# Cross attention's layer norm computed inside the down projection before it, and the first batch's tiles loaded there

## The chip, the cores and the metric

One core of a Trainium2 chip runs the whole program. The metric is the device time of one execution in microseconds. The kernel before has a median of 2226.97 us in three runs (2225.14 to 2232.52).

## The reference

Eight batches of 256 tokens with 512 features pass through two gated blocks. Each block adds a gated attention and a gated feed-forward part to x. The change lies between the end of the first block and the start of the second:

```python
x = x + jnp.tanh(g_xattn[0]) * _L0_xattn_ref(_layernorm(x, axis=-1), ctx_2048, ...)
x = x + jnp.tanh(g_ffn[0]) * _L0_ffn_ref(_layernorm(x, axis=-1), L0_ffn_w_gate, L0_ffn_w_up, L0_ffn_w_down)
x = x + jnp.tanh(g_xattn[1]) * _L1_xattn_ref(_layernorm(x, axis=-1), ctx_2048, ctx_2048)
x = x + jnp.tanh(g_ffn[1]) * _L1_ffn_ref(_layernorm(x, axis=-1), L1_ffn_w1, ...)

def _layernorm(x, axis=-1, eps=1e-05):
    m = jnp.mean(x, axis=axis, keepdims=True)
    v = jnp.var(x, axis=axis, keepdims=True)
    return (x - m) / jnp.sqrt(v + eps)
```

`_L0_ffn_ref` ends in `h_sparse @ w_down`, 2048 features down to 512. `_L1_xattn_ref` is causal attention with 16 heads of 32 features: queries are the normalised x, keys and values both the context, and the scores are divided by sqrt(32).

## The kernel before, in words

Seven stages run one after the other. Each is a block with one program per engine, and an all-engine barrier closes it. Between stages x goes through DRAM. Batches are taken in four pairs of 512 tokens, which are 16 tiles of 128 tokens.

**The down projection (stage 5, `down` with tag `d_`, lines 1073 to 1319).** The loop goes over the 16 token tiles g. Two of the products were already computed in stage 4. For each of the 14 others ScalarE rounds the tile to its high part (L1270), VectorE takes the low part (L1302), and TensorE adds up 48 products of 128x128 by 128x512 (L258 to L260). VectorE then adds gate times product to x (`add`, L1286), and SyncE stores y (L1164). SyncE has the only DMA queue and works in program order: load tile g, load one piece of the weights of stage 7, store an old y, load an old x. Eight pieces of 1 MB pass through four buffers `raw`. ScalarE takes a piece's signs, VectorE sums its sizes (L1306), and TensorE turns the signs in between. GpSimd has nothing to do in this stage.

**The cross stage (stage 6, `cross`, lines 1633 to 2061).** A batch has 16 heads, taken as eight pairs p, and an engine's program is a chain of steps, one pair a step. In step p TensorE computes the scores of pair p (L1848, L1851), turns the probabilities of pairs p-2 and p-1 (L1860) and in even steps multiplies by the values (L1875). VectorE masks (L2008) and takes the maximum (L2012), ScalarE takes exp (L1937, L1939) and copies the turned probabilities out of PSUM (L1950). Two PSUM banks S hold scores, so the scores of pair p wait for the exps of pair p-2. Work on the neighbouring batches is hung into fixed steps: outputs of the batch before in steps 3 and 4 (L1885, L2033, then GpSimd's adds L1799), and for the batch after the statistics of its layer norm in step 2 (L192 to L197), its normalising in step 4 (L204) and its turning into queries in steps 5 and 6 (L1830, copied by L1930 and L1998). The power -1/2 of the variance is GpSimd's (L213).

Before the first step the stage loads the first batch's x (`x_xl`, L1747) and its keys (`x_kt`, L1750), normalises, turns and copies. TensorE first runs 12 throw-away products on the identity (`keep_awake`, L253) once x has landed, and 12 more in each of the first two steps. One such f32 product stands in the trace as two rows, so a dozen is x24. Ahead of all of it VectorE fills `x_masked` and the two whole score banks with a constant (L1989, L1991), and TensorE waits for that.

Of the kernel before, what the change touches and what calls it, by code (L numbers as in the profile page):

```python
# [1072 lines left out]
def down(nc, io, c, scr, tag, w, gate, x_from, x_to):  # L1073
# [4 lines left out]
    with ExitStack() as ctx:  # L1078
# [35 lines left out]
        if made:  # L1114
            SIGNS = 8
            AHEAD = 4
            raw = [mem.sb(f"raw{i}", [P, 4, 512]) for i in range(WP)]
# [4 lines left out]
            W = mem.bank("W")  # L1122
            v_arrived = [mem.sem(f"v_arrived{i}") for i in range(SIGNS)]
# [21 lines left out]
        def piece(n):  # L1145
            return raw[n % WP][:].rearrange("p k n -> p (k n)")

        @block.sync
        def _(sp):
# [16 lines left out]
            def load_piece(n):  # L1166
                if n >= WP:
                    sp.wait_ge(signed, n - WP + 1)
                    sp.wait_ge(summed, n - WP + 1)
                src = W1[:, 4 * n:4 * n + 4, :] if n < 4 else W2[:, n - 4, :].rearrange("p (o d) -> p o d", o=4)  # L1170
                sp.dma_start(raw[n % WP][:], src).then_inc(v_arrived[n], 16)
# [11 lines left out]
            for g in range(QUICK, N):  # L1183
                load_a(g)
                for n in ([0, 1] if made and g == QUICK else coming(g, -2)):
                    load_piece(n)
                if g >= 3:
                    store_y(g - 3)
                    if g + 1 < N:
                        load_x(g + 1)  # L1190
            for g in range(N - 3, N):
                store_y(g)
            for s in y_stored:
                sp.wait_ge(s, 16 * PAIRS)

# [84 lines left out]
        def _(dve):  # L1280
# [7 lines left out]

            for j in range(WP):
# [7 lines left out]
                elif j == 0:  # L1297
                    add(0)
            for g in range(QUICK, N):
# [3 lines left out]
                                  ALU.subtract).then_inc(lo_done, 1)  # L1303
                for n in coming(g):
# [8 lines left out]
            if made:  # L1313
                dve.wait_ge(W_sum, 1)
# [3 lines left out]
                dve.tensor_tensor(c.gain2[:], c.wmean[:, 1:2], c.gates[:, 3:4], ALU.mult).then_inc(summed, 1)  # L1318
            add(N - 1)

# [312 lines left out]
def cross(nc, io, c, scr):  # L1633
# [7 lines left out]
    with ExitStack() as ctx:  # L1641
# [8 lines left out]
        xl = mem.sb("xl", [P, QT, D])  # L1650
# [3 lines left out]
        kt = [mem.sb(f"kt{b}", [P, DC, L]) for b in range(2)]  # L1654
# [51 lines left out]
        ln = LayerNorm(mem, xl_arrived, xl, spread=HD1, tiles=QT, parts=2)  # L1706
# [31 lines left out]
        def _(sp):  # L1738
# [4 lines left out]
            def load(turn, b):  # L1743

                own = slice(QT * b, QT * (b + 1))
                wait_apart(sp, ln.xn_ready, turn, QT * b, passed)
                sp.dma_start(xl[:], scr.x[1][turn, :, own, :]).then_inc(xl_arrived.sem, 16)  # L1747
                wait_apart(sp, S_full, turn, BP * (b - 1), passed)
                for stands in range(2):
                    sp.dma_start(kt[b][:, :, stands * P:(stands + 1) * P],  # L1750
                                 scr.ct[turn, :, :, b * L + (1 - stands) * P:b * L + (2 - stands) * P]
                                 ).then_inc(kt_arrived[b].sem, 16)
                wait_apart(sp, PV_done, turn, BQ * (b - 1), passed)
# [16 lines left out]
            load(0, 0)  # L1770
# [5 lines left out]
        def _(pool):  # L1776
            for s in (ln.rstd_ready, ev_done, xe_done, y_done):
                s.start(pool)
# [23 lines left out]
            def step(i, at, batch):  # L1802
                if i == 2:
                    for turn, b in batch(1):
                        ln.gpsimd(pool, turn, c.minus_half, b)
# [7 lines left out]
            ln.gpsimd(pool, 0, c.minus_half, 0)  # L1813
# [3 lines left out]
        def _(pe):  # L1817
# [4 lines left out]
            def turn_x(turn, b, t):  # L1822
                pe.wait_ge(*ln.xn_ready.at(turn, QT * b + t + 1))
                if t == 0:
                    pe.wait_ge(*o_done.at(turn, QT * (b - 1)))
# [3 lines left out]
                for k in range(DC):  # L1829
                    last = pe.transpose(M[:, k * P:(k + 1) * P], ln.xn[:, t, k * P:(k + 1) * P], c.ident[:])  # L1830
# [85 lines left out]
            pe.wait_ge(*xl_arrived.at(0, 16))  # L1916
            keep_awake(pe, O, c, AWAKE)
# [67 lines left out]
        def _(dve):  # L1985
            for s in (x_kept[1], v1_kept, masked_done, max_done, sums_done, rsum_done, gain_done, apart_gained, o_done,
                      ln.stats, ln.xn_ready):
# [49 lines left out]
            def step(i, at, batch):  # L2037
# [7 lines left out]
                if i == 2:  # L2045
                    for turn, b in batch(1):
                        ln.statistics(dve, turn, b)
# [3 lines left out]
                if i == 4:  # L2051
                    for turn, b in batch(1):
                        ln.normalise(dve, turn, X_full.at(turn, QT * b), b)
# [4 lines left out]
            ln.statistics(dve, 0, 0)  # L2058
            ln.normalise(dve, 0, X_full.at(0, 0), 0)
# [364 lines left out]
class Consts:  # L2424
# [26 lines left out]
    def make_last(self, nc):  # L2451
# [8 lines left out]
        self.gain2 = far("gain2", [P, 1])  # L2460


class Scratch:


    def __init__(self, nc, kind="Internal"):
# [11 lines left out]
        self.bias = dram("bias_parts", [3, INNER], BF16)  # L2478
        self.x = [dram(f"x_after{i}", [PAIRS, P, TT, D]) for i in range(3)]
# [70 lines left out]
```

## Time and profile before

| | |
|---|---|
| median of three runs | 2226.97 us |
| the profiled execution, its own time | 2230.12 us |
| its span | 2228.3 us |
| TensorE busy (matmul) | 1992.4 us, 89% |
| VectorE busy | 1370.8 us, 62% |
| ScalarE busy | 1073.8 us, 48% |
| GpSimd busy | 426.5 us, 19% |
| stage 5 | about 1634 to 1810 us |
| stage 6 | about 1811 to 2050 us |

Times in the rows are microseconds from the start of the span unless they are marked ns. TensorE is PE (its weight loads PEld), VectorE is DVE, ScalarE ACT, GpSimd POOL and SyncE SP. L with a number is the line of the kernel before. A matmul's end is modelled and overlaps the next one, so intervals between starts are the safer measure on TensorE. The clock is a share of 2.4 GHz: 0.5 is the lower of TensorE's two levels, 1.2 GHz.

### The profile page before, as it was taken

How to read it: one execution, taken by the hardware profiler on the slowest of the kernel's cores; microseconds unless marked ns; L12 is line 12 of the kernel's file. 1: busy time of each engine (PE TensorE's matmuls, PEld its weight loads, DVE VectorE, ACT ScalarE, POOL GpSimd, SP SyncE). 2: the span in 40 equal slices, each digit the busy share in tenths (PEclk: the TensorE clock that was granted, in tenths of full speed). 3: DMA queues.
4: the chain of work that ended last, by engine and by line, in shares of the span. 5: the costliest groups of instructions: out<-in, count | busy, mean ns of one | idle time of the engine just before them, and what ended most of it. 6: DMA issues, size and time to landing. Idle time of an engine off the chain costs nothing. (4 is left out here: it accounts for less than half of the span.)

```text
span 2228.3 us, 33499 instructions
## 1 busy us (share of the span) xinstructions
PE 1992.4 (89%) x10778; PEld 1527.1 (69%) x10794; DVE 1370.8 (62%) x2397; ACT 1073.8 (48%) x2590; POOL 426.5 (19%) x504
## 2 busy tenths in 40 slices
PE   6999479999989999987997989999979979997898
PEld 5888357777767777765886868787768866665454
DVE  6777366666666767664223764555644338885786
ACT  3333156665656666663112611122224318885898
POOL 1111034444444444430000000000000001222110
PEclk9999789999999999998999999999989989998999
DMA  5665662324232231016442321212375322221111
GB/s 215 245 245 228 250 180 76 89 74 105 58 105 77 77 86 48 20 29 224 152 144 88 120 57 57 75 38 76 114 280 192 118 82 86 96 95 49 49 57 43
DMA packets 191785, 250.41 MB, mean 112 GB/s; under 512 B 11526, under 2 KB 143766, under 8 KB 181276
## 3 DMA queue, kind: packets, MB, share of 16 engines
q1 hardware_dynamic: 191644, 248.67, 34.1%
q8 instruction: 72, 1.18, 0.2%
q14 instruction: 69, 0.57, 0.1%
HBM read 152.14 MB, written 96.48 MB: 112 GB/s over the span
## 5 line engine op out<-in xcount | busy, mean ns | idle before, releaser
L937 ACT ACTIVATE at_prob<-at_S,at_bias,at_rq 128x384 f32<-128x384 f32 (+1 forms) x256 | 184.3, 731 | 165.6 <-DVE at_bias L1023 155.2
L1034 DVE TENSOR_TENSOR at_pt_lo<-at_PT,at_pt_hi 128x512 fp32r<-128x512 f32 x224 | 148.9, 689 | 92.5 <-ACT at_pt_hi L944 92.5
L805 POOL TENSOR_SCALAR at_prob<-at_prob,at_rsum 128x384 f32<-128x384 f32 (+1 forms) x256 | 161.2, 643 | 174.5 <-DVE at_rsum L1029 174.4
L864 PE MATMUL at_PT<-c_ident,at_prob 128*128 128x128 f32 x896 | 127.8, 277 | 45.1 <-DVE at_pt_lo L1034 45.1
L1527 ACT ACTIVATE gu_silu<-gu_G 128x512 f32<-128x512 f32 x64 | 38.2, 598 | 243.3 <-PE gu_G L103 233.7
L944 ACT ACTIVATE at_pt_hi<-at_PT 128x512 fp32r<-128x512 f32 x224 | 128.0, 604 | 52.9 <-PE at_PT L864 52.9
L1014 DVE TENSOR_REDUCE at_nmax<-at_S 128x1 f32<-128x384 f32 (+1 forms) x256 | 147.6, 616 | 4.6 <-PE at_S L857 4.1
L864 PEld LDWEIGHTS at_PT<-c_ident,at_prob 128*128 128x128 f32 x896 | 97.7, 140 | 76.6 <-DVE at_pt_lo L1034 72.3
L1565 DVE TENSOR_TENSOR gu_h<-gu_silu,gu_U 128x512 f32<-128x512 f32 x64 | 43.9, 687 | 142.9 <-PE gu_U L103 96.1
L853 PE MATMUL at_S<-at_k_hi,at_q_hi 128*128 128x384 f32 (+1 forms) x256 | 112.6, 440 | 16.4 <-DVE at_q_lo L1039 13.4
L796 POOL TENSOR_TENSOR at_rq<-at_qv,c_minus_half 128x4 f32<-128x4 f32 x64 | 65.2, 1019 | 287.0 <-DVE at_qv L1009 287.0
L101 PE MATMUL at_Q<-at_wq_hi,at_xt_hi 128*128 128x512 f32 x256 | 107.8, 421 | 6.3 <-issue 3.5
L258 PE MATMUL down_Y<-down_w_hi,down_a_hi 128*128 128x512 f32 x256 | 102.3, 400 | 11.9 <-DVE d_y L1286 11.9
L213 POOL TENSOR_TENSOR x_rstd<-x_ve,c_minus_half 128x2 f32<-128x2 f32 x8 | 8.9, 1117 | 503.1 <-DVE x_ve L197 503.1
L103 PE MATMUL at_Q<-at_wq_lo,at_xt_hi 128*128 128x512 f32 x256 | 102.9, 402 | 0.0
L102 PE MATMUL at_Q<-at_wq_hi,at_xt_lo 128*128 128x512 f32 x256 | 102.3, 400 | 0.0
L258 PE MATMUL o_Y<-o_w_hi,o_a_hi 128*128 128x512 f32 x256 | 99.8, 390 | 1.7 <-DVE o_a_lo L1302 1.7
L260 PE MATMUL down_Y<-down_w_lo,down_a_hi 128*128 128x512 f32 x256 | 100.9, 394 | 0.0
L259 PE MATMUL down_Y<-down_w_hi,down_a_lo 128*128 128x512 f32 x256 | 100.9, 394 | 0.0
L260 PE MATMUL o_Y<-o_w_lo,o_a_hi 128*128 128x512 f32 x256 | 99.6, 389 | 0.0
L259 PE MATMUL o_Y<-o_w_hi,o_a_lo 128*128 128x512 f32 x256 | 99.6, 389 | 0.0
L101 PE MATMUL at_O<-at_pt_hi,at_v_hi 128*128 128x512 f32 x224 | 99.0, 442 | 0.5 <-DVE at_pt_lo L1034 0.4
(306 smaller groups left out, 5661.6 us busy)
## 6 DMA issues: line engine op xcount, KB each, us to landing
wide<-at_ot SPq DMA_DIRECT2D x64, 256.0 KB, 2.8
wide<-gu_h SPq DMA_DIRECT2D x64, 256.0 KB, 3.2
o_a<-wide SPq DMA_DIRECT2D x14, 1024.0 KB, 4.8
d_a<-wide SPq DMA_DIRECT2D x13, 1024.0 KB, 4.8
keys_hi<-kv_kt_hi SPq DMA_DIRECT2D x8, 1024.0 KB, 4.0
keys_lo<-kv_kt_lo SPq DMA_DIRECT2D x8, 1024.0 KB, 6.0
values_hi<-kv_v_hi SPq DMA_DIRECT2D x8, 1024.0 KB, 8.0
values_lo<-kv_v_lo SPq DMA_DIRECT2D x8, 1024.0 KB, 9.6
```

The costliest lines, as they stand in the source:

```text
L101: pe.matmul(out, wh, xh, start=(start and k == 0), stop=False)
L103: last = pe.matmul(out, wh, xl, start=False, stop=(stop and k == len(terms) - 1))
L258: pe.matmul(Y[:], a_hi[:, k, :], w_hi[:, k, :], start=(k == 0), stop=False)
L259: pe.matmul(Y[:], a_lo[:, k, :], w_hi[:, k, :], start=False, stop=False)
L260: return pe.matmul(Y[:], a_hi[:, k, :], w_lo[:, k, :], start=False, stop=(k == IC - 1))
L805: pool.tensor_scalar(prob[u % 2][:, h, 0:n], prob[u % 2][:, h, 0:n], rsum[:, s:s + 1], 1.0, ALU.mult, ALU.mult).then_inc(normed.sem, 1)
L853: pe.matmul(S[h][:, 0:n], q_hi[u % 2][:, own], keys, start=True, stop=False)
L864: last = pe.transpose(bank_of("p", u, kb)[:, h * P:(h + 1) * P], prob[u % 2][:, h, kb * P:(kb + 1) * P], c.ident[:])
L937: act.activation(prob[u % 2][:, h, 0:n], S[h][:, 0:n], ACT.Exp, bias=bias[:, s:s + 1], scale=rq[u % 4][:, h:h + 1], accum_out=sums[:, s:s ...
L944: act.activation(pt_hi[f % 4][:], bank_of("p", u, kb)[:], ACT.Copy).then_inc(pt_hi_done.sem, 1)
L1014: dve.tensor_reduce(nmax[:, s:s + 1], S[h][:, 0:blocks[u] * P], AX_X, ALU.max, negate=True).then_inc(max_done.sem, 1)
L1034: dve.tensor_tensor(pt_lo[f % 4][:], bank_of("p", u, kb)[:], pt_hi[f % 4][:].bitcast(F32), ALU.subtract).then_inc(pt_done.sem, 1)
```

## The change

Stage 5 now also computes the layer norm of stage 6. After the low part of tile g, VectorE normalises tile g-3 and takes the statistics of tile g-2, and GpSimd takes the power. The normalised tiles go to a new DRAM array `x_normalised`, two buffers deep, through SyncE's queue. At g = 12 SyncE loads the first batch's normalised x and keys into two tiles, `xl` and `kt0`, that outlive the stage. Four buffers for weight pieces become three. In stage 6 the layer norm goes from VectorE and GpSimd in every batch, TensorE turns `xl` itself, its first dozen throw-away products goes, and only the part of the score banks that no product writes is filled. The load of the next `xl` waits for the turning of the last one instead of for its normalising.

```diff
@@ down @@
+            RAW = 3
+            raw = [mem.sb(f"raw{i}", [P, 4, 512]) for i in range(RAW)]
...
             def load_piece(n):
-                if n >= WP:
-                    sp.wait_ge(signed, n - WP + 1)
-                    sp.wait_ge(summed, n - WP + 1)
+                if n >= RAW:
+                    sp.wait_ge(signed, n - RAW + 1)
+                    sp.wait_ge(summed, n - RAW + 1)
...
+            def store_xn(g):
+                sp.wait_ge(xn_done, g + 1)
+                sp.dma_start(scr.xn[g // TT, :, g % TT, :], xn[:, g % 2, :]).then_inc(xn_stored[g % 2], 16)
+            def load_ahead():
+                for r in range(2):
+                    sp.wait_ge(xn_stored[r], 16)
+                sp.dma_start(c.xl[:], scr.xn[0, :, 0:2, :]).then_inc(ahead_arrived, 16)
+                for stands in range(2):
+                    sp.dma_start(c.kt0[:, :, stands * P:(stands + 1) * P],
+                                 scr.ct[0, :, :, (1 - stands) * P:(2 - stands) * P]).then_inc(ahead_arrived, 16)
...
+                if made and g >= 4:
+                    store_xn(g - 4)
+                if made and g == N - 4:
+                    load_ahead()
             for g in range(N - 3, N):
                 store_y(g)
+                if made:
+                    store_xn(g - 1)
+            if made:
+                store_xn(N - 1)
+                for s in xn_stored:
+                    sp.wait_ge(s, 16 * N // 2)
+                sp.wait_ge(ahead_arrived, 3 * 16)
...
+                    pool.tensor_tensor(rstd[:, r], ve[:, r], c.minus_half[:, 0:1], ALU.pow).then_inc(rstd_done, 1)
...
+            def statistics(g):
+                r = g % 2
+                dve.wait_ge(y_done, g + 1)
+                dve.bn_stats(bn[:, r, :], y[:, g % TT, :]).then_inc(bn_done, 1)
+                dve.wait_ge(bn_done, 2 * g + 1)
+                dve.bn_aggr(mv[:, r, :], bn[:, r, :]).then_inc(bn_done, 1)
+                dve.wait_ge(bn_done, 2 * g + 2)
...
+                dve.tensor_scalar(ve[:, r:r + 1], mv[:, r, 1:2], EPS_LN, float(HD1), ALU.add, ALU.mult).then_inc(ve_done, 1)
+            def normalise(g):
...
+                dve.tensor_scalar(xn[:, r, :], y[:, g % TT, :], mv[:, r, 0:1], rstd[:, r:r + 1], ALU.subtract,
+                                  ALU.mult).then_inc(xn_done, 1)
...
             add(N - 1)
+            if made:
+                statistics(N - 1)
+                normalise(N - 1)
@@ cross @@
-                wait_apart(sp, ln.xn_ready, turn, QT * b, passed)
-                sp.dma_start(xl[:], scr.x[1][turn, :, own, :]).then_inc(xl_arrived.sem, 16)
+                wait_apart(sp, X_full, turn, QT * b, passed)
+                sp.dma_start(xl[:], scr.xn[turn, :, own, :]).then_inc(xl_arrived.sem, 16)
...
-            load(0, 0)
+            sp.sem_inc(xl_arrived.sem, 16)
+            sp.sem_inc(kt_arrived[0].sem, 32)
+            load_values(0, 0)
...
-                    last = pe.transpose(M[:, k * P:(k + 1) * P], ln.xn[:, t, k * P:(k + 1) * P], c.ident[:])
+                    last = pe.transpose(M[:, k * P:(k + 1) * P], xl[:, t, k * P:(k + 1) * P], c.ident[:])
...
-            pe.wait_ge(*xl_arrived.at(0, 16))
-            keep_awake(pe, O, c, AWAKE)
...
-                dve.memset(S[i][:], MASKED_L1).then_inc(masks, 1)
+                unseen = S[i][:].rearrange("p (a l) -> p a l", a=2)[:, :, P:L]
+                dve.memset(unseen, MASKED_L1).then_inc(masks, 1)
...
-                if i == 2:
-                    for turn, b in batch(1):
-                        ln.statistics(dve, turn, b)
...
-                if i == 4:
-                    for turn, b in batch(1):
-                        ln.normalise(dve, turn, X_full.at(turn, QT * b), b)
...
-            ln.statistics(dve, 0, 0)
-            ln.normalise(dve, 0, X_full.at(0, 0), 0)
```

Three places show how the instructions move. The first is VectorE at the end of stage 5 and the start of stage 6, before the change (`last_` names are constants for stage 7):

```order
L1286 SCALAR_TENSOR_TENSOR d_y<-down_Y,c_gates,d_x 128x512
L1078 UNCONDITIONAL_BRANCH
L1984 UNCONDITIONAL_BRANCH
L1989 MEMSET x_masked 128x512
L1991 MEMSET x_S 128x1024 x2
L192 BN_STATS x_bn<-x_xl 128x6 x2
L195 BN_AGGR x_mv<-x_bn 128x2 x2
L197 TENSOR_SCALAR x_ve<-x_mv 128x2
L204 TENSOR_SCALAR x_xn<-x_xl,x_mv,x_rstd 128x512 x2
L1998 COPY x_qt<-x_M 128x4x128
```

The same place after it:

```order
L1332 SCALAR_TENSOR_TENSOR d_y<-down_Y,c_gates,d_x 128x512
L1339 BN_STATS d_bn<-d_y 128x6
L1341 BN_AGGR d_mv<-d_bn 128x2
L1345 TENSOR_SCALAR d_ve<-d_mv 128x1
L1352 TENSOR_SCALAR d_xn<-d_y,d_mv,d_rstd 128x512
L1078 UNCONDITIONAL_BRANCH
L2060 UNCONDITIONAL_BRANCH
L2064 MEMSET x_masked 128x512
L2067 MEMSET x_S 128x2x128 x2
L2074 COPY x_qt<-x_M 128x4x128
```

The layer norm of the last tile now stands ahead of the stage's end, and none stands behind it. The second place is TensorE at the start of stage 6, before and after:

```order
L1816 UNCONDITIONAL_BRANCH
L253 MATMUL x_O<-c_ident 128x128 x12
L1830 MATMUL x_M<-c_ident,x_xn 128x128 x8
L1848 MATMUL x_S<-x_kt,x_qt 128x128 x2
L1851 MATMUL x_S<-x_kt,x_qt 128x256 x2
L253 MATMUL x_O<-c_ident 128x128 x12
```

```order
L1894 UNCONDITIONAL_BRANCH
L1908 MATMUL x_M<-c_ident,last_xl 128x128 x8
L1926 MATMUL x_S<-last_kt,x_qt 128x128 x2
L1929 MATMUL x_S<-last_kt,x_qt 128x256 x2
L253 MATMUL x_O<-c_ident 128x128 x12
```

The dozen ahead of the turning is gone, the dozen behind the first scores stays. The third place is SyncE's queue in one tile of stage 5, before and after:

```order
L1155 DMA d_a<-wide 128x2048
L1171 DMA d_raw<-in_L_ffn_w_dram 128x2048
L1164 DMA x_after<-d_y 128x512
L1160 DMA d_x<-x_after 128x512
L1155 DMA d_a<-wide 128x2048
```

```order
L1167 DMA d_a<-wide 128x2048
L1183 DMA d_raw<-in_L_ffn_w_dram 128x2048
L1176 DMA x_after<-d_y 128x512
L1172 DMA d_x<-x_after 128x512
L1187 DMA x_normalised<-d_xn 128x512
L1167 DMA d_a<-wide 128x2048
```

One more store stands between two loads of `d_a`.

## Rows read from the trace of the kernel before

**Rows 1.** Busy time by stretch, then TensorE's granted clock, DMA share, GB/s.

```profile
1641.00:1807.00 166.00, 164.41 (x802) 133.54 (x802) 60.72 (x43) 55.37 (x54) 0.00 (x0) 0.98 0.50 180
1816.00:1822.00 6.00, 5.22 (x24) 5.25 (x25) 2.78 (x7) 0.00 (x0) 0.70 (x1) 0.50 0.55 177
```

**Rows 2.** Waits of stage 5: us in total, times, longest.

```profile
PE down_Y L258 <- DVE d_y L1286: 11.9, 1, 11.9
```

**Rows 3.** Timeline, end of stage 5, start of stage 6: start, us, instruction, [idle before].

```profile
1807.17 0.75 DVE L1286 SCALAR_TENSOR_TENSOR d_y<-down_Y,c_gates,d_x 128x512 f32<-128x512 f32 x1 [10.11 <-PE down_Y L260]
...
1807.95 0.33 SPq L1164 DMA_DIRECT2D x_after<-d_y  x1
...
1812.55 0.48 DVE L1989 MEMSET x_masked<- 128x512 f32 x1 [4.64 <-issue]
...
1813.25 0.91 DVE L1991 MEMSET x_S<- 128x1024 f32 x1 [0.21 <-issue]
...
1816.78 5.46 PE L253 MATMUL x_O<-c_ident 128*128 128x128 f32 x24 [9.75 <-DMA x_xl<-x_after]
...
1818.81 0.70 POOL L213 TENSOR_TENSOR x_rstd<-x_ve,c_minus_half 128x2 f32<-128x2 f32 x1 [362.60 <-DVE x_ve L197]
...
1822.03 0.73 PE L1830 MATMUL x_M<-c_ident,x_xn 128*128 128x128 f32 x4
...
1825.05 0.49 PE L1848 MATMUL x_S<-x_kt,x_qt 32*128 32x128 f32 x4 [0.83 <-issue]
```

**Rows 4.** Timeline of TensorE, the two dozens behind the first scores.

```profile
1826.06 4.38 PE L253 MATMUL x_O<-c_ident 128*128 128x128 f32 x24
...
1831.22 2.94 PE L253 MATMUL x_O<-c_ident 128*128 128x128 f32 x24
```

**Rows 5.** VectorE's layer norm in stage 6: count, busy us, mean ns, idle before.

```profile
L192 DVE BATCH_NORM_STATS2 x_bn<-x_xl 128x6 f32<-128x512 f32 x16 | 10.2, 680 | 1.5 <-DMA x_xl<-x_after 1.5
...
L195 DVE BATCH_NORM_AGGREGATE x_mv<-x_bn 128x2 f32<-128x6 f32 x16 | 2.6, 182 | 1.2 <-DVE x_bn L192 0.5
...
L197 DVE TENSOR_SCALAR x_ve<-x_mv 128x2 f32<-128x2 f32 x8 | 1.4, 170 | 0.3
```

**Rows 6.** The range of the normalising and of GpSimd's power, ns min/median/max.

```profile
L204 DVE TENSOR_SCALAR x_xn<-x_xl,x_mv,x_rstd x16: 537/818/1504, 1819.5 to 2003.6; 128x512 f32<-128x512 f32 x16
L213 POOL TENSOR_TENSOR x_rstd<-x_ve,c_minus_half x8: 697/1174/1219, 1818.8 to 1997.3; 128x2 f32<-128x2 f32 x8
```

**Rows 7.** TensorE's first score product of steps 6 and 7, batch 0.

```profile
1847.81 0.49 PE L1848 MATMUL x_S<-x_kt,x_qt 32*128 32x128 f32 x4 [0.40 <-ACT x_prob L1939]
...
1851.38 0.49 PE L1848 MATMUL x_S<-x_kt,x_qt 32*128 32x128 f32 x4
```

**Rows 8.** The same two of batch 1, first of six alike.

```profile
1873.61 0.49 PE L1848 MATMUL x_S<-x_kt,x_qt 32*128 32x128 f32 x4 [0.23 <-ACT x_prob L1939]
...
1877.91 0.49 PE L1848 MATMUL x_S<-x_kt,x_qt 32*128 32x128 f32 x4 [0.20 <-ACT x_prob L1939]
```

**Rows 9.** Timeline of batch 6, the last of the six, from step 4 to 7.

```profile
2003.17 1.95 DVE L204 TENSOR_SCALAR x_xn<-x_xl,x_mv,x_rstd 128x512 f32<-128x512 f32 x2
...
2004.85 0.49 PE L1848 MATMUL x_S<-x_kt,x_qt 32*128 32x128 f32 x4 [0.21 <-ACT x_prob L1939]
...
2007.03 0.37 ACT L1937 ACTIVATE x_prob<-x_S,x_nmax 128x128 f32<-128x128 f32 x1 [1.36 <-DVE x_nmax L2012]
...
2009.18 0.49 PE L1848 MATMUL x_S<-x_kt,x_qt 32*128 32x128 f32 x4 [0.20 <-ACT x_prob L1939]
```

**Rows 10.** Batch 7, in which no layer norm stands: VectorE's longest mask.

```profile
2029.43 1.64 DVE L2008 COPY_PREDICATED x_S<-x_after,x_masked 128x512 f32<-128x512 int32 x1 [0.27 <-PE x_S L1851]
```

**Rows 11.** Loads of stage 5: an issue, the rounding that uses it, landing of all.

```profile
1660.75 0.33 SPq L1155 DMA_DIRECT2D d_a<-wide  x1
...
1678.80 1.92 ACT L1270 ACTIVATE down_a_hi<-d_a 128x2048 fp32r<-128x2048 f32 x1 [7.73 <-PE down_Y L260]
...
DMA to landing us min/median/max: 3.5/4.8/12.0
```

More of the change, by code:

```diff
@@ L1122, in down @@
             W = mem.bank("W")
+            xn = mem.sb("xn", [P, 2, D])
+            bn = mem.sb("bn", [P, 2, 6])
+            mv = mem.sb("mv", [P, 2, 2])
+            ve = mem.sb("ve", [P, 2])
+            rstd = mem.sb("rstd", [P, 2])
+            bn_done = mem.sem("bn_done")
+            ve_done = mem.sem("ve_done")
+            rstd_done = mem.sem("rstd_done")
+            xn_done = mem.sem("xn_done")
+            xn_stored = [mem.sem(f"xn_stored{r}") for r in range(2)]
+            ahead_arrived = mem.sem("ahead_arrived")
             v_arrived = [mem.sem(f"v_arrived{i}") for i in range(SIGNS)]
@@ L1190, in _ @@
                         load_x(g + 1)
+                if made and g >= 4:
+                    store_xn(g - 4)
+                if made and g == N - 4:
+                    load_ahead()
             for g in range(N - 3, N):
                 store_y(g)
+                if made:
[5 more added lines that the diff above has]
+                sp.wait_ge(ahead_arrived, 3 * 16)
             for s in y_stored:
                 sp.wait_ge(s, 16 * PAIRS)
+        if made:
+            @block.gpsimd
+            def _(pool):
+                for g in range(N):
+                    r = slice(g % 2, g % 2 + 1)
+                    pool.wait_ge(ve_done, g + 1)
+                    if g >= 2:
+                        pool.wait_ge(xn_done, g - 1)
+                    pool.tensor_tensor(rstd[:, r], ve[:, r], c.minus_half[:, 0:1], ALU.pow).then_inc(rstd_done, 1)
         @block.tensor
@@ L1298, in _ @@
                     add(0)
+            if made:
+                statistics(0)
             for g in range(QUICK, N):
@@ L1303, in _ @@
                                   ALU.subtract).then_inc(lo_done, 1)
+                if made:
+                    normalise(g - 3)
+                    statistics(g - 2)
                 for n in coming(g):
@@ L1313, in _ @@
             if made:
+                normalise(N - 3)
+                statistics(N - 2)
                 dve.wait_ge(W_sum, 1)
@@ L1318, in _ @@
                 dve.tensor_tensor(c.gain2[:], c.wmean[:, 1:2], c.gates[:, 3:4], ALU.mult).then_inc(summed, 1)
+                normalise(N - 2)
             add(N - 1)
+            if made:
+                statistics(N - 1)
+                normalise(N - 1)
 def gate_up(nc, io, c, scr):
@@ L1653, in cross @@
         qt = [mem.sb(f"qt{b}", [P, DC, L]) for b in range(2)]
-        kt = [mem.sb(f"kt{b}", [P, DC, L]) for b in range(2)]
+        kt = [c.kt0, mem.sb("kt1", [P, DC, L])]
         prob = [mem.sb(f"prob{i}", [P, 3 * P]) for i in range(4)]
@@ L1752, in load, with load_values @@
                                  ).then_inc(kt_arrived[b].sem, 16)
+                load_values(turn, b)
+            def load_values(turn, b):
+                own = slice(QT * b, QT * (b + 1))
                 wait_apart(sp, PV_done, turn, BQ * (b - 1), passed)
@@ L1776, in _ @@
         def _(pool):
-            for s in (ln.rstd_ready, ev_done, xe_done, y_done):
+            for s in (ev_done, xe_done, y_done):
                 s.start(pool)
```

26 lines of the change are left out of this document (14 added, 12 removed).

## The prediction, made before the changed kernel ran

> **What bounds the kernel now.** I read the busy times by stretch first. In the loop of stage 5, 1641 to 1807 us, TensorE is busy 164.41 of 166.00 us and VectorE 60.72, at a clock of 0.98 [rows 1]. The waits of that stage name one wait of TensorE on VectorE, 11.9 us, once, at its start [rows 2]. So the stage is TensorE's, and work added to VectorE there has room: 166.00 - 60.72 = 105 us are free over 13 tiles, some 8 us a tile.
>
> The timeline across the border comes second [rows 3]. The last add begins at 1807.17 and ends at 1807.92, the store of y is issued at 1807.95, VectorE's first instruction of stage 6 stands at 1812.55 (4.60 later), TensorE's throw-away dozen starts at 1816.78 when x has landed, the turning at 1822.03 and the first scores at 1825.05. From the store to the first scores 17.10 us pass in which nothing of use runs on TensorE but eight transposes. The layer norm itself is hidden there: it lies beside the dozen, 1816.78 to 1822.24. What can go from the path is the landing and the dozen, not the layer norm.
>
> Third, the steps of stage 6. I take the start of the first score product of each step. Steps 6 to 7 took 1851.38 - 1847.81 = 3.57 in batch 0 [rows 7], which has no outputs of a batch before it and whose normalising met no adds of GpSimd. In the six batches 1 to 6 the same step took 4.30 in the first [rows 8] and 4.33 in the last [rows 9], 4.09, 4.00, 4.08 and 3.99 between, 24.79 in all. In batch 6 the normalising holds VectorE 1.95 us from 2003.17, and after it ScalarE waits 1.36 us for a maximum at 2007.03 [rows 9]. The other steps agree between the batches within 0.1 us.
>
> **The change part by part.** All positions from here are us behind the issue of the last y store.
>
> *The stage's end gets longer.* Behind the last add now stand, one after the other: statistics 0.68, aggregate 0.18, scale 0.17 [rows 5], GpSimd's power 0.70 [rows 3] and the normalising 0.54 [rows 6], 2.27 in all. Five hand-overs join them (VectorE's wait on its own add, two inside the statistics, to GpSimd and back). I estimate 0.1 each, with the gap of 0.21 at 1813.25 [rows 3] as the upper end: 2.8. SyncE then has some five more semaphores to pass before the barrier, estimated 0.2. I take T = 3.0. No engine works beside it, so I take the short durations. The upper bound uses the medians of the busy stage, 1.17 for the power and 0.82 for the normalising [rows 6]: 3.8. The lower, with hand-overs of 0.05, is 2.7. The landing of the last store and the barrier stay as they are, 4.60 less 0.2 for two counters that VectorE no longer starts: 4.4.
>
> *The stage's start gets shorter.* The mask tile 0.48, gap 0.21, then two fills of 256 instead of 1024 columns. One of 1024 took 0.91 [rows 3]. In proportion 256 take 0.23, and with a fixed part I take 0.28 (bounds 0.23 and 0.91). With a gap between: 0.48 + 0.21 + 0.28 + 0.16 + 0.28 = 1.4. TensorE's own waits 0.5. Turning starts at 4.4 + 1.4 + 0.5 = 6.3. From turning to first scores was 1825.05 - 1822.03 = 3.02 [rows 3]. There the array had just come to full clock, now it comes out of idleness. In the dozen at the low level a product starts every 5.46 / 24 = 0.23 us, in the last one every 2.94 / 24 = 0.12 [rows 3, 4]. Two groups of four transposes become some 0.5 longer each: 4.0. The first scores start at 10.3 + T = 13.3 instead of 17.1: 3.8 us earlier. The loads of xl and keys that left this place land during stage 5, where the DMA share was 0.50 [rows 1].
>
> *What the missing dozen costs later.* The granted clock was 0.50 in 1816 to 1822 [rows 1]. The dozen behind the first scores took 4.38, between the 5.46 of a slow one and the 2.94 of a fast one [rows 3, 4], so the clock had fallen again and rose inside it. Without the first dozen it may rise later. At best nothing changes, at worst this dozen is slow throughout, 1.1 more, the scores 0.3 more, and the next dozen is slow too, 5.46 - 2.94 = 2.5 more: 0 to 3.9. I take 0.5, as the products from the turning onward still run. The border gives 3.8 - 0.5 = 3.3 us.
>
> *The Trainium skill against this edit.* The row shows 0.50 after the idle time at the border [rows 1]. TensorE: Matmul & The Clock Gate, Part 1: The HAM clock gate, says that the idle array is throttled by default and only activity releases it. The trace agrees. By that rule the removed dozen was not waste, and the case in which it is missed is the second rival below.
>
> *Steps of stage 6.* Statistics and normalising leave VectorE in seven batches. Statistics show no price: step 2 to 3 took what batch 7 needs without them. The normalising shows one, in step 6. Down to batch 0's 3.57, six steps give back 24.79 - 6 x 3.57 = 3.4. Batch 0 had no output work and no adds of GpSimd in the way, so the floor may lie higher. In batch 7, without any layer norm, a mask took 1.64, beside an add of GpSimd [rows 10]: it then hits the mask instead. I take 3.1, bounds 0 and 3.9 (all small excesses of other steps too).
>
> SBUF — State Buffer, Who interferes with whom, says that a VectorE instruction with two SBUF inputs contends with a GpSimd instruction that reads SBUF. The trace agrees. By it the gain might be passed on to the mask and be lost, which is the first rival.
>
> *In the loop of stage 5.* VectorE gets 0.68 + 0.18 + 0.17 + 0.54 and semaphores, about 2.1 us a tile, into the 8 free. The low part stands ahead of it in the queue, and behind it only the sums of a weight piece, whose users are tiles away. GpSimd was idle. SyncE gets 16 stores of 0.35 us issue, three loads, and an earlier stop: with three buffers a piece's load waits for the sum of the piece three back, which ends in the tile before, and y's store, x's load and the next load of `d_a` queue behind it. That `d_a` load is issued at some 1665 instead of 1660.75. Its user starts at 1678.80, so it had 18.05 us for a landing of 4.8, 12.0 at most [rows 11]. 4 us less are hidden. Cost 0, bounds 0 and 1.
>
> **Sum.** -3.3 - 3.1 = -6.4 us. Against the profiled execution 2230.12 becomes 2223.7. That execution lies 3.1 above the median of the runs, 2226.97, so the median becomes 2220.6, 0.29% less. What a measurement of this kernel can tell from no change is about 0.3%, or 6.7 us: the forecast lies at that line.
>
> **The rivals.**
>
> *The steps do not move.* TensorE's own work or the mask behind GpSimd's adds fills the room of the normalising. For it: rows 10. Against it: batch 7's other steps are no longer than those of batches 1 to 6. Only the border is left: 2226.97 - 3.3 = 2223.7. Chance 0.14.
>
> *The array stays slow.* Both later dozens run at the low level: 3.9 instead of 0.5, so -6.4 + 3.4 = -3.0 and 2224.0. For it: a dozen was not enough to keep the clock before [rows 4]. Against it: the products that made it rise in that dozen are still there. Chance 0.08.
>
> *More comes back.* The fills cost 0.23, the clock nothing (0.5 + 0.1), T is 2.7 (0.3), and the steps fall to 3.57 with their small excesses (0.8): -6.4 - 1.7 = -8.1, 2218.9. Chance 0.14.
>
> *Slower: SyncE's queue in stage 5.* Its place is the load of `d_a` behind a piece that waits for a sum. It decides from the point where the load comes more than 18.05 us less the landing too late: with the longest landing, 12.0, that is 6 us [rows 11]. The piece wait brings 4; waits for the xn store or longer landings from the added traffic would have to bring the rest. Five tiles (pieces 3 to 7) pay what is over it. At 3 us each, -6.4 + 15 = +8.6, 2235.6. For it: the stage once waited 11.9 us at its start with many loads in flight [rows 2]. Against it: the usual landing leaves 9 us. Chance 0.07.
>
> That the change does not do what it says, because the layer norm just moves to the end of stage 5, is in T: only the last tile's does.
>
> **How the numbers follow.** The forecast has 0.57, the rivals 0.14, 0.08, 0.14 and 0.07. Of the forecast's own range, 2217.5 to 2223.5, somewhat less than half lies under 2220.3: 0.26 faster, 0.31 the same. Faster by over 0.3%: 0.26 + 0.14 = 0.40. Within: 0.31 + 0.14 + 0.08 = 0.53. Slower: 0.07. The range is 2216.5 to 2226: it leaves out the slower case and some at the low end.
>
> **What would show it.** In the profile after: TensorE idle from the last product to the first transpose for about 10.2 us (6.3 + T + the 0.9 from its end to the y store), the first scores 13.3 us behind the store of the last y; step 6 of batches 1 to 6 near 3.6; stage 5's loop at 166 us with no new wait of TensorE; GpSimd's power in the tail near 0.70. Wrong would be: a wait of TensorE on `down_a_lo` or of ScalarE on `d_a` in stage 5, steps of 4 us as before, or dozens that take over 5 us twice.

## The result, and the profile after

| | before | after |
|---|---|---|
| median of the runs, us | 2230.93 (20 runs) | 2224.36 (20 runs) |
| profiled span, us | 2228.3 | 2222.5 |
| profiled execution's own time, us | 2230.12 | 2224.63 |

Both were timed together on one chip. The ratio of after to before is 0.9976, 95% interval 0.9968 to 0.9985: 0.24% faster, some 5.4 us. The medians differ by 6.6. The forecast was -6.4 us, or 2220.6, with a range of 2216.5 to 2226. Its distance to 2224.36, 3.8 us, is the level of the day: the kernel before took 2230.93 here and 2226.97 when the forecast was made, 4.0 more.

The border first, in the timeline of after (start, us, instruction, idle before). It answers to [rows 3]:

```profile
1807.13 0.75 DVE L1332 SCALAR_TENSOR_TENSOR d_y<-down_Y,c_gates,d_x 128x512 f32<-128x512 f32 x1 [7.71 <-PE down_Y L260]
1807.91 0.33 SPq L1176 DMA_DIRECT2D x_after<-d_y  x1
1807.92 0.69 DVE L1339 BATCH_NORM_STATS2 d_bn<-d_y 128x6 f32<-128x512 f32 x1
...
1808.65 0.18 DVE L1341 BATCH_NORM_AGGREGATE d_mv<-d_bn 128x2 f32<-128x6 f32 x1
1808.87 0.15 DVE L1345 TENSOR_SCALAR d_ve<-d_mv 128x1 f32<-128x1 f32 x1
1809.10 0.54 POOL L1240 TENSOR_TENSOR d_rstd<-d_ve,c_minus_half 128x1 f32<-128x1 f32 x1 [10.26 <-DVE d_ve L1345]
1809.68 0.55 DVE L1352 TENSOR_SCALAR d_xn<-d_y,d_mv,d_rstd 128x512 f32<-128x512 f32 x1 [0.66 <-POOL d_rstd L1240]
...
1814.82 0.48 DVE L2064 MEMSET x_masked<- 128x512 f32 x1 [4.60 <-issue]
...
1815.36 0.55 DVE L2067 MEMSET x_S<- 128x256 f32 x2
...
1815.96 1.12 PE L1908 MATMUL x_M<-c_ident,last_xl 128*128 128x128 f32 x4 [8.96 <-DVE x_S L2067]
...
1817.82 1.12 PE L1908 MATMUL x_M<-c_ident,last_xl 128*128 128x128 f32 x4 [0.74 <-ACT x_qt L2006]
...
1819.94 0.80 PE L1926 MATMUL x_S<-last_kt,x_qt 32*128 32x128 f32 x4 [1.01 <-issue]
...
1821.53 4.32 PE L253 MATMUL x_O<-c_ident 128*128 128x128 f32 x24
```

From the store of the last y to the first scores 12.03 us pass (1819.94 - 1807.91), where it was 17.10: 5.07 less. The layer norm of the last tile stands open ahead of the barrier, as forecast. The turning takes 1.12 us for four transposes; at full clock they take 0.60 (in the run no early load, below). The array comes out of its idle time at the low level and stays there until the dozen of step 0:

```profile
1810.80:1824.40 13.60, 6.69 (x29) 5.27 (x30) 3.64 (x6) 2.54 (x5) 0.00 (x0) 0.50 0.47 149
```

This row is a stretch, its length, the busy times of five engines, then the granted clock (0.50), DMA share and GB/s. Step 0 of the first batch, from its first scores to the next ones, takes 5.83 us (5.32 before).

Then step 6, as the start of its first score product and of step 7's, batch 1 and then batch 6. They answer to [rows 8, 9]; between them an add of GpSimd and a mask of VectorE in batch 1:

```profile
1866.85 1.28 POOL L1881 TENSOR_TENSOR x_y<-x_o,x_x 128x512 f32<-128x512 f32 x1 [2.49 <-DVE x_o L2109]
1867.04 1.65 DVE L2084 COPY_PREDICATED x_S<-x_after,x_masked 128x512 f32<-128x512 int32 x1 [0.27 <-PE x_S L1929]
...
1869.01 0.49 PE L1926 MATMUL x_S<-x_kt,x_qt 32*128 32x128 f32 x4 [0.40 <-ACT x_prob L2015]
...
1872.58 0.49 PE L1926 MATMUL x_S<-x_kt,x_qt 32*128 32x128 f32 x4
...
1997.63 0.49 PE L1926 MATMUL x_S<-last_kt,x_qt 32*128 32x128 f32 x4 [0.40 <-ACT x_prob L2015]
...
2001.20 0.49 PE L1926 MATMUL x_S<-last_kt,x_qt 32*128 32x128 f32 x4
```

Step 6 takes 3.57 in all of batches 1 to 6, 21.42 together against 24.80 (the forecast has 24.79, from rounded terms): 3.38 less. TensorE's wait is 0.40 for ScalarE, as in the undisturbed batch 0 [rows 7]. The rival's mechanism is in the rows too: the add beside it stretches the mask from 0.70 to 1.65 us. It costs nothing, since VectorE has slack without the layer norm.

The loop of stage 5, by stretch (columns as in [rows 1]), and its waits:

```profile
1641.00:1807.00 166.00, 163.39 (x802) 132.78 (x802) 81.76 (x103) 56.12 (x55) 8.15 (x15) 0.98 0.61 210
```

```profile
ACT down_a_hi L1316 <- DMA d_a<-wide: 12.7, 2, 7.7
...
PE down_Y L258 <- DVE d_y L1332: 11.0, 1, 11.0
```

VectorE took 21 us more, GpSimd 8, the DMA share rose from 0.50 to 0.61, and TensorE's only wait is the one at the start [rows 2]. ScalarE waited for `d_a` twice, 12.7 us in all. The prediction named such a wait as a sign of being wrong, but the kernel before has one too, of 5.0 us. The median landing of a `d_a` load rose from 4.8 to 7.5 us. TensorE paid nothing for either: no wait of TensorE for what ScalarE makes of `d_a` stands in the list.

So the stages up to the end of stage 6 gained 5.07 - 0.51 + 3.38 = 7.94 us, but the span only 5.8. The last stage gave back 2.1: from the last store of stage 6 to the end 180.8 us before, 182.9 after. No line of its code was touched. Stretches of 10 us from that store on, the third and the fourth, of before and then of after. The columns are the stretch, its length, five engines' busy times, the granted clock, DMA share and GB/s:

```profile
2067.50:2077.50 10.00, 7.05 (x35) 3.11 (x34) 7.63 (x29) 8.98 (x13) 1.64 (x3) 0.97 0.01 2
2077.50:2087.50 10.00, 7.39 (x43) 3.49 (x42) 8.44 (x30) 9.97 (x14) 1.48 (x2) 0.83 0.01 2
```

```profile
2059.60:2069.60 10.00, 7.05 (x29) 2.81 (x28) 7.72 (x28) 9.19 (x12) 2.41 (x3) 0.84 0.06 21
2069.60:2079.60 10.00, 7.94 (x45) 3.77 (x44) 7.39 (x21) 8.94 (x12) 1.48 (x2) 0.84 0.01 2
```

After has a second stretch at part of the clock, 0.84 and 0.84 where before had 0.97 and 0.83. The stretches ahead of them read 0.50 and 0.67 in both. The early stages differ too: +2.3 us at the start of stage 4, back again by the end of stage 5. Two traces of the same kernel before differ there by 3.4, so a difference of this size says nothing of the change.

### The profile page after: what moved, and what is told of

It reads as the page before. It is cut to its first block and busy times, and to the rows that moved or that the text cites. A ratio compares the mean times of both kernels' runs of the same rounds, so it can differ in the third digit from the quotient of the medians.

```text
span 2222.5 us, 33491 instructions
## 1 busy us (share of the span) xinstructions
PE 1992.8 (90%) x10770; PEld 1523.6 (69%) x10770; DVE 1377.9 (62%) x2405; ACT 1075.7 (48%) x2590; POOL 424.1 (19%) x512
## 5 line engine op out<-in xcount | busy, mean ns | idle before, releaser
L855 PE MATMUL at_S<-at_k_hi,at_q_lo 128*128 128x384 f32 (+1 forms) x256 | 94.2, 368 | 0.0
```

## The experiments

All lengths below are from one trace each, in us. Border is from the store of the last y to the first scores, 0 and 1 are the first two steps of batch 0, 6 is the sum of step 6 over batches 1 to 6, last is the last stage. The traces of down only and no early load are of the slowest of their ten executions, with 8.0 and 6.0 us more ahead of the last y store than before, so their spans say little.

| kernel | border | 0 | 1 | 6 | last | span | ratio to before (95%) |
|---|---|---|---|---|---|---|---|
| before | 17.10 | 5.32 | 5.14 | 24.80 | 180.8 | 2228.3 | 1 |
| before again | 17.22 | 5.33 | 5.14 | 24.75 | 180.7 | 2232.0 | 0.9992 (0.9977 to 1.0006) |
| after | 12.03 | 5.83 | 5.14 | 21.42 | 182.9 | 2222.5 | 0.9976 (0.9968 to 0.9985) |
| after again | 12.02 | 5.75 | 5.14 | 21.42 | 182.8 | 2222.6 | 0.9976 (0.9965 to 0.9988) |
| down only | 20.59 | 5.31 | 5.14 | 24.74 | 181.0 | 2239.9 | 1.0015 (1.0001 to 1.0029) |
| no early load | 19.62 | 6.90 | 5.15 | 21.42 | 181.9 | 2235.8 | 1.0008 (0.9994 to 1.0021) |
| dozen back | 16.68 | 5.32 | 5.14 | 21.42 | 181.0 | 2227.4 | 0.9984 (0.9973 to 0.9995) |
| statistics back | 12.11 | 6.42 | 5.14 | 21.42 | 181.9 | 2224.9 | 0.9970 (0.9955 to 0.9986) |
| normalising back | 12.14 | 5.92 | 5.14 | 22.40 | 182.7 | 2223.1 | 0.9964 (0.9949 to 0.9979) |
| both back | 12.21 | 6.20 | 5.14 | 24.76 | 181.9 | 2228.0 | 0.9990 (0.9981 to 0.9999) |
| bridge | 12.03 | 6.54 | 5.14 | 21.42 | 180.1 | 2222.3 | 0.9955 (0.9938 to 0.9972) |
| bridge, short dozens | 12.02 | 4.44 | 4.85 | 21.42 | 180.9 | 2218.6 | 0.9942 (0.9924 to 0.9959) |
| short dozens | 12.02 | 4.44 | 6.60 | 21.42 | 181.4 | 2221.0 | 0.9966 (0.9953 to 0.9980) |
| shorter dozens | 12.02 | 2.73 | 6.36 | 21.42 | 178.7 | 2219.1 | 0.9962 (0.9947 to 0.9976) |

**Before and after again**, unchanged.

> The kernel before, profiled a second time, as the measure of how far one profiled execution differs from the next, stage by stage. Theory: the gain is the border of stages 5 and 6 (4.6 us net) and step 6 of batches 1 to 6 (3.4 us), 8.0 us, and the 2.2 us by which the profiled difference (5.8 us) falls short came from stage 7 (181 us from the last store of stage 6 before, 183 after), whose length scatters from run to run. Then here: 17.1 us from the last y store of stage 5 to the first scores within 0.3, step 6 at 4.0 to 4.3, and stage 7 somewhere between 180.5 and 183. Rival: stage 7 is longer because of the change (other tile addresses, another phase of the clock). Then stage 7 is 180.8 within 0.3 here, and 183 in every profile of the changed kernel.

> The changed kernel, profiled a second time and timed in five rounds. Theory: border 12.0 us from the last y store to the first scores within 0.5, step 0 of batch 0 at 5.3 to 6.3, step 6 at 3.57 in every batch, stage 7 between 180.5 and 183.5, 5 to 8 us faster than the kernel before in the median. Rival (stage 7 pays for it): stage 7 at 183 again and 5.4 us.

The border and the steps repeat within 0.12 us, so a difference of 0.3 in them means something. The last stage repeats as well, 0.1 apart for each kernel. So the theory that its 2.1 us are scatter from run to run fell, and the rival held: they come with the changed kernel as it stands.

**The parts of the border.** Down only has stage 5 of after, without the early loads, and the whole stage 6 of before.

```diff
-                if made and g == N - 4:
-                    load_ahead()
...
-                sp.wait_ge(ahead_arrived, 3 * 16)
```

> Only the work added to stage 5: its layer norm, the stores of the normalised tiles and three piece buffers, without the early loads; stage 6 is that of the kernel before, so the layer norm is computed twice. Theory: the loop of stage 5 stays as long as before, the stage's end grows by T, measured as 2.35 us in the changed kernel, and nothing else moves: +2 to +3 us. Rival (the queue of SyncE delays loads and costs in the loop): ScalarE waits for d_a and TensorE stands idle in tiles 5 to 9, +5 us or more.

No early load takes after, and loads the first batch behind the barrier, with the first dozen back to cover the wait.

```diff
-                if made and g == N - 4:
-                    load_ahead()
-                sp.wait_ge(ahead_arrived, 3 * 16)
...
-            sp.sem_inc(xl_arrived.sem, 16)
-            sp.sem_inc(kt_arrived[0].sem, 32)
-            load_values(0, 0)
+            load(0, 0)
...
+            pe.wait_ge(*xl_arrived.at(0, 16))
+            keep_awake(pe, O, c, AWAKE)
```

> The change without the early loads: stage 6 loads its first batch's normalised x and keys itself and runs the first dozen throw-away products once they have landed, as before; the layer norm is gone from stage 6. Theory: the border is then 17.1 + 2.35 = 19.5 us, no shorter, since the layer norm was hidden beside the dozen; step 6 is 3.57; in sum +2.4 - 3.4 = -1 us. Rival (the layer norm itself was on the path at the border): the border is 17 us or less and the sum -4 us.

Dozen back has the early load and the first dozen.

```diff
+            keep_awake(pe, O, c, AWAKE)
             for t in range(QT):
                 turn_x(0, 0, t)
```

> The changed kernel with the first dozen of throw-away products put back ahead of the turning, as in the kernel before. Theory A (the removed dozen was on the path): the turning starts 4 to 5.5 us later, a dozen at half clock, the first scores stand 15.5 to 17 us behind the last y store instead of 12.0, and step 0 shortens by at most 0.5 us to 5.3: 3 to 5 us above the changed kernel. Theory B (its absence is paid for in the dozens behind it): steps 0 and 1 shorten by 2 us or more, and the time is within 2 us of the changed kernel.

Read as a ladder, the border goes 17.10, 20.59 (layer norm at the end of stage 5: +3.5), 19.62 (none in stage 6, smaller fills: -1.0), 16.68 (early load: -2.9), 12.03 (no dozen: -4.7). Of the +3.5, 2.5 lie between the last add and the first fill. Another 0.8 is the landing of x behind it, which after does not wait for.

The border alone misleads at two rungs, because step 0 moves too. In no early load step 0 takes 6.90 us. There the clock rose at the end of the first dozen and fell again just as the first scores began. The turning ran fast, and the dozen behind the scores ran at the low level throughout:

```profile
1830.60 0.60 PE L1903 MATMUL x_M<-c_ident,last_xl 128*128 128x128 f32 x4
...
1835.09 5.49 PE L253 MATMUL x_O<-c_ident 128*128 128x128 f32 x24
```

Border and step 0 together go 22.42, 25.90 (+3.5), 26.52 (+0.6), 22.00 (early load: -4.5), 17.86 (no dozen: -4.1). The early load and the missing dozen are of like size, so the gain of this border is not the dozen's alone. A kernel without the dozen and without the early load was not run. Over border, step 0 and step 6 no early load stands 0.7 above before, where -1 was expected.

The loop of stage 5, from the first add to the last product, stays at 163.6 to 165.1 us in all kernels (164.9 before), so the stores and the three buffers cost it nothing. Down only was expected at +2 to +3 us and came to +3.5 at the border, with no wait in the loop: the rival on SyncE's queue failed there too. TensorE in dozen back:

```profile
1818.64 5.49 PE L253 MATMUL x_O<-c_ident 128*128 128x128 f32 x24 [8.95 <-DVE x_S L2068]
1823.92 0.96 PE L1908 MATMUL x_M<-c_ident,last_xl 128*128 128x128 f32 x4
1825.62 0.66 PE L1908 MATMUL x_M<-c_ident,last_xl 128*128 128x128 f32 x4 [0.74 <-ACT x_qt L2007]
1827.29 0.49 PE L1926 MATMUL x_S<-last_kt,x_qt 32*128 32x128 f32 x4 [1.01 <-issue]
1827.59 0.66 PE L1929 MATMUL x_S<-last_kt,x_qt 32*128 32x256 f32 x4
1828.18 4.50 PE L253 MATMUL x_O<-c_ident 128*128 128x128 f32 x24
```

It runs 5.49 us at the low level. The scores behind it start at full clock, 0.49 for four against 0.80 in after, and the next dozen takes 4.50 against 4.32. From turning to scores the dozen buys 0.6 (3.37 instead of 3.98) and in step 0 0.5, for 5.3 us on the path. Theory A held.

**The parts of step 6.** Each of these gives after's stage 6 some of its layer norm back, on `xl`, with a result that no product uses. First the statistics with GpSimd's power, at step 2:

```diff
+                if i == 2:
+                    for turn, b in batch(1):
+                        dve.wait_ge(*ln.rstd_ready.at(turn, b))
+                        ln.statistics(dve, turn, b)
```

> The changed kernel with the statistics of the layer norm (two BN_STATS, two BN_AGGR, one scale on VectorE in step 2, one power on GpSimd) put back into stage 6 on the same tiles, their results unused. Theory: only the normalising delayed step 6, so step 6 stays at 3.57 and the batches at 25.7. Rival (any 2 us on VectorE count): step 6 or step 3 grows by 0.4 or more per batch. For stage 7, which took 182.8 to 182.9 us from the last store of stage 6 in both profiles of the changed kernel and 180.7 to 181.0 in three profiles of kernels with the old stage 6: if GpSimd's and VectorE's layer norm work decides it, it falls back towards 181 here; if not, it stays at 182 to 183.

Then the normalising alone, at step 4, with constant scalars and without GpSimd's power:

```diff
+                if i == 4:
+                    for a in batch(1):
+                        norm_back(*a)
```

> The changed kernel with two normalising instructions (TENSOR_SCALAR of 128x512) put back into step 4 of stage 6, with constant scalars and an unused result; no statistics. Theory: step 6 of batches 1 to 6 is back at 4.0 to 4.3, since GpSimd's adds and the normalising meet (VectorE held some 2 us), 25.7 becomes 26.1 to 26.5 a batch, 3 us in all. Rival (the delay needs the statistics and the power too, which push GpSimd's adds into the normalising): step 6 stays at 3.57.

Neither brings the old step back. The statistics cost nothing (21.42), the normalising 0.98 (22.40), where 3.38 had been won. So the theory that the normalising alone made the step long fell short, and the last one put both back:

```diff
+                if i == 2:
+                    for turn, b in batch(1):
+                        ln.statistics(dve, turn, b)
...
+                if i == 4:
+                    for turn, b in batch(1):
+                        ln.normalise(dve, turn, ln.xn_ready.at(turn, QT * b), b)
```

> The changed kernel with the whole layer norm (statistics, GpSimd's power, normalising) done once more in stage 6 at its old steps, on the tile that the early load brought; what it computes is not used by the products. Theory A (VectorE's and GpSimd's work of the layer norm together made step 6 long): step 6 of batches 1 to 6 goes back to 4.0 to 4.3 us each, 24 to 25 us in all, and the border stays within 1 us of 12.0; the time is some 3 us above the changed kernel. Theory B (something else than the layer norm gave it back, such as the place of the first loads or the clock): step 6 stays at or under 3.8 us in all, as it did with the normalising alone.

The six steps are 4.30, 4.08, 3.99, 4.08, 3.98 and 4.33 again. VectorE in batch 6 shows how two prices of 0 and 0.98 make 3.34. Normalising alone:

```profile
1988.70 1.23 DVE L2092 TENSOR_REDUCE x_nmax<-x_S 128x4 f32<-128x1024 f32 x1
1990.26 0.70 DVE L2088 COPY_PREDICATED x_S<-x_after,x_masked 128x512 f32<-128x512 int32 x1 [0.33 <-PE x_S L1931]
...
1993.39 1.43 DVE L2088 COPY_PREDICATED x_S<-x_after,x_masked 128x512 f32<-128x512 int32 x1 [0.56 <-PE x_S L1931]
...
1996.59 1.96 DVE L2121 TENSOR_SCALAR x_xn<-last_xl,x_mv,x_rstd 128x512 f32<-128x512 f32 x2
```

Both back:

```profile
1993.19 1.22 DVE L2094 TENSOR_REDUCE x_nmax<-x_S 128x4 f32<-128x1024 f32 x1
1994.33 1.27 DVE L192 BATCH_NORM_STATS2 x_bn<-last_xl 128x6 f32<-128x512 f32 x2
...
1996.24 0.70 DVE L2090 COPY_PREDICATED x_S<-x_after,x_masked 128x512 f32<-128x512 int32 x1
...
1998.71 1.72 DVE L2090 COPY_PREDICATED x_S<-x_after,x_masked 128x512 f32<-128x512 int32 x1
...
2002.20 1.95 DVE L204 TENSOR_SCALAR x_xn<-last_xl,x_mv,x_rstd 128x512 f32<-128x512 f32 x2
```

Alone, VectorE sits idle 0.33 and 0.56 us ahead of two masks, and the normalising starts 16.74 us behind the batch's first scores (1996.59 - 1979.85). With the statistics both idle times are gone and it starts 17.39 behind them (2002.20 - 1984.81), 0.65 later. Step 6 is 4.33 instead of 3.68, the same 0.65. The statistics use up VectorE's slack, and the normalising then has none to hide in. That is shown for the pair. It is not shown for VectorE's statistics alone: both back also has GpSimd's power, which moves its adds, and the longest mask there is 1.72 instead of 1.43. No run has the normalising with only one of the two.

**The dozens that remain.** Four kernels ask what the clock after the border is worth. Bridge puts throw-away products at the end of stage 5 and four in front of the turning:

```diff
+            if made:
+                pe.wait_ge(summed, SIGNS + 4)
+                keep_awake(pe, W, c, 22)
...
+            keep_awake(pe, O, c, 4)
```

> The changed kernel with throw-away products over the border: 22 behind stage 5's last product, while VectorE and SyncE finish, and 4 at the start of stage 6 while VectorE fills. Theory: TensorE idled 9 us at the border and came out at half clock; bridged, the turning takes 0.73 instead of 1.12 twice, the scores 1.0 instead of 1.6, step 0 falls from 5.8 to 3.8, steps 0 and 1 together from 10.9 to 9.0 and the first scores come 1.2 us earlier: 3 us less in all. Rival (the 2 us of the barrier between are enough for the clock to fall, or the products hold up the barrier): the first scores 12.0 behind the last y store or later and step 0 above 5.

The second bridge also cuts the dozens of steps 0 and 1 to 6 and 8:

```diff
-                    keep_awake(pe, O, c, AWAKE)
+                    keep_awake(pe, O, c, 6 if i == 0 else 8)
```

> As the bridge, and the dozens of steps 0 and 1 cut to 6 and 8 products. Theory: at full clock the scores, the 6, the scores and the 8 end near 5.3 us behind the first scores, when the first exps are ready (5.3 in the changed kernel), so steps 0 and 1 take 7 instead of 10.9 us: 5 us less than the changed kernel. Rival (the clock falls in the waits that the dozens filled): steps 0 to 3 come at half clock and the gain is under 2 us.

Short dozens has that edit alone, without the bridge.

> The changed kernel with the two remaining dozens of throw-away products (steps 0 and 1 of the first batch) cut from 24 products to 6 and 8, and no products across the border. Theory A (those dozens are on the path and the products across the border were worth nothing): steps 0 and 1 take 9.0 to 9.5 us together instead of 11.0, 1.7 us less than the changed kernel. Theory B (the products across the border helped): the two steps take over 10 us, and the time is that of the changed kernel.

Shorter dozens goes further, again without it.

```diff
-                    keep_awake(pe, O, c, AWAKE)
+                    keep_awake(pe, O, c, 2 if i == 0 else 4)
```

> As the one before, the dozens cut to 2 and 4 products. Theory A (what the steps wait for sets a floor of their own, the scores to maximum to exponentials chain): steps 0 and 1 take 7.5 to 8.8 us together and nothing is lost later, 2.5 us less than the changed kernel. Theory B (the dozens hold the clock up): the granted clock stays low into the steps behind them, and steps 2 and 3 become longer by 1 to 3 us, so that nothing or less is won.

The bridge was expected to win 3 us and the second one 5. In bridge the array still fell to the low level:

```profile
1809.41 5.07 PE L253 MATMUL d_W<-c_ident 128*128 128x128 f32 x44
1817.36 1.22 PE L253 MATMUL x_O<-c_ident 128*128 128x128 f32 x8 [2.87 <-PEq L127]
1818.54 1.12 PE L1912 MATMUL x_M<-c_ident,last_xl 128*128 128x128 f32 x4
```

The 44 rows are the 22 products at the end of stage 5, in 5.07 us at full clock. Behind 2.87 us of idle time come the four products of stage 6, and then the turning at the low level. The clock did not fall in the idle time, though. It fell 0.9 us after the products had resumed, as three stretches show:

```profile
1814.40:1817.30 2.90, 0.09 (x1) 0.00 (x0) 0.00 (x0) 0.00 (x0) 0.00 (x0) 1.00 0.01 4
1817.36:1818.20 0.84, 0.84 (x7) 0.84 (x8) 0.75 (x2) 0.00 (x0) 0.00 (x0) 1.00 0.17 47
1818.30:1828.40 10.10, 8.35 (x38) 6.69 (x37) 2.80 (x4) 3.60 (x10) 0.00 (x0) 0.50 0.71 214
```

It came back 6.0 us behind the first scores, in after 4.5. So step 0 was longer, 6.54, not shorter, and the span that of after: nothing won by the bridge alone. Cutting the dozens alone won nothing either, 4.44 + 6.60 = 11.04 against 10.97, because the clock rose late. Step 1 with short dozens:

```profile
1826.50 3.67 PE L253 MATMUL x_O<-c_ident 128*128 128x128 f32 x16
```

and with the bridge:

```profile
1826.19 2.05 PE L253 MATMUL x_O<-c_ident 128*128 128x128 f32 x16
```

The same sixteen rows, eight products, take 3.67 or 2.05 us. Beside short dozens the bridge wins 11.04 - 9.29 = 1.75, so theory A of short dozens, by which it was worth nothing, fell. The 9.29 are still far from the 7 that had been expected of both edits. Shorter dozens alone reach 9.09, just above the 7.5 to 8.8 expected. Their steps 2 to 5 stay at 12.29 us, so no product there was slowed, and theory B fell. The bridge is thus not needed for this gain. The version with the bridge and dozens of 6 and 8 took 2220.93 us by median, over four runs. Its ratio of 0.9942 has an interval that lies wholly below after's, and so beats both kernels. But of the 3.9 us between its span and that of after 1.7 lie in steps 0 and 1, and 2.0 in the last stage. The intervals of the other three overlap after's. Differences of 1 us between such ratios can't be read.

**The last stage.** No experiment was made for it alone, but fourteen traces speak. It runs 178.7 to 182.9 us with the same code, and its length goes neither by the border nor by the layer norm in stage 6. A small part does: its first load is issued 4.28 us behind the last store in the five traces with the statistics in stage 6, and 4.55 to 4.58 behind it in the others, 0.3 of the 2.1. In shorter dozens, the shortest, the third and fourth stretch read:

```profile
2060.40:2070.40 10.00, 6.78 (x33) 2.75 (x31) 7.92 (x30) 9.05 (x13) 1.47 (x2) 0.99 0.01 2
2070.40:2080.40 10.00, 7.83 (x51) 4.16 (x53) 8.57 (x26) 9.97 (x14) 1.48 (x2) 1.00 0.00 0
```

No stretch at part of the clock there, one in before, two in after: 178.7, 180.8, 182.9. Over the first 60 us of the stage the granted clock is 0.86 in shorter dozens and 0.85 in bridge (178.7 and 180.1 us). It is 0.83 in five traces of 180.7 to 181.1, 0.81 in two of 181.4 and 181.9, and 0.80 in the three of 182.7 to 182.9. Only statistics back and both back leave this order, with 0.83 and 181.9. So the length goes with the clock. What makes the clock fall there in one kernel and not in another stays open.

## Why the prediction came out right

**T, the stage's end.** Forecast 3.0, less 0.2 for two counters: 2.8 from the last add to the first fill. Measured 2.3. The last add ends at 1807.88 and the first fill of stage 6 stands at 1814.82, 6.94 later; before it was 4.63. The five instructions take 0.69 + 0.18 + 0.15 + 0.54 + 0.55 = 2.11 (forecast 2.27), and the hand-overs 0.04 to 0.08 each, 0.24 together, where I had 0.1 each. The 0.2 for SyncE's semaphores did not show, nor did the 0.2 for the counters (4.59 from the normalising's end to the first fill, 4.63 before).

**The stage's start.** Two fills take 0.55 together, 0.28 each as forecast. The gaps of 0.21 and 0.16 ahead of them were 0.06 and nothing, and TensorE started 0.05 behind the last one instead of 0.5. From the first fill to the turning it was 1.14, forecast 1.9. From turning to scores 3.98, forecast 4.0. Border: -5.07, forecast -3.8. The difference is 0.5 up to the first fill and 0.8 from there to the turning. TensorE stood idle 8.96 us ahead of it, where 10.2 had been forecast.

**The missing dozen.** Forecast 0.5, measured 0.51. The dozen behind the scores took 4.32, no longer than the 4.38 before [rows 4]. The 0.5 is in the scores themselves, 0.80 and 1.09 us for four. I had put it on the dozen.

By the Trainium skill (TensorE: Matmul & The Clock Gate, Part 1: The HAM clock gate) an idle array is throttled and activity releases it. One pair of runs agrees: beside short dozens, the bridge's products let step 1 run at full clock, 2.05 against 3.67. The other pair does not: with the full dozens, the clock rose later in bridge than in after. The rule does not say that a dozen pays, and here it cost 5.3 us for a gain of 1.1.

**Steps of stage 6.** Forecast -3.1, measured -3.38, with the floor of 3.57 exact. The size was right, and the reason half right. The prediction's "Statistics show no price" read a batch in which the normalising was missing too. Statistics and power have one when the normalising is there: 24.76 with all of it, 22.40 with the normalising alone.

By the Trainium skill (SBUF — State Buffer, Who interferes with whom) a VectorE instruction with two inputs in SBUF contends with a GpSimd instruction that reads SBUF. The mask of 1.65 beside an add agrees. The rival built on it failed: the step did not lengthen.

**Stage 5.** Forecast 0, measured 0. The rival on SyncE's queue is refuted as to cost: no wait of TensorE, and a loop as long as before in every kernel with the three buffers. ScalarE's wait for `d_a` did grow, from 5.0 to 12.7 us, and was hidden.

**The sum.** Forecast -6.4. The terms came to -4.56 and -3.38, -7.94: what I had as the rival "More comes back", -8.1. The time moved by 5.4 to 6.6, since the last stage took 2.1 of it. The sum had no term for a stage behind the change. So the forecast was near by luck: two errors, of 1.5 and 2.1 us, cancel. What held is the way, that border and step 6 both gain, and the size of each within 1.3 us.

## What to carry to other kernels

Cover for an idle array has to be priced like any work on the path: here a dozen throw-away products at half clock cost 5.3 us and sped up what followed by 1.1. A part of a border is priced only with the step behind it, which can take back what the border gained. Two operations that share an engine's slack have no price each, so take away or put back both before naming a culprit. And where a stage's clock is not steady, a gain ahead of it can change it by 2 us either way. Compare stages between fixed events, and not spans alone.

## What the hardware showed that I had not expected

- In both bridges the clock was still full over 2.87 and 2.84 us of idle time and fell 0.9 and 0.7 us after products had resumed.
- Behind the early load and without the first dozen, the turning never ran at full clock, and the clock rose at different places behind it: inside the dozen of step 0 in after, only at the end of step 1's products with short dozens.
- A hand-over between VectorE and GpSimd, or of VectorE to itself, showed as 0.04 to 0.08 us in the rows.
- GpSimd's power took 0.54 us on one column with nothing beside it, 0.70 on two [rows 3].
- A mask of VectorE beside an add of GpSimd took 1.65 instead of 0.70 us in after, and cost the step nothing.
